# Graph layers: degrees reordered and repeated through DRAM instead of by products on TensorE

## The reference, cut to what matters

```python
# second block (_gcn_norm): degrees by target, with self-loops
deg = jax.ops.segment_sum(jnp.ones_like(col, jnp.float32), col, num_segments=n)
dis = jnp.where(deg > 0, jax.lax.rsqrt(jnp.maximum(deg, 1.0)), 0.0)
norm = dis[row] * dis[col]
...
h = x @ W
msg = h[row] * norm[:, None]
out = jax.ops.segment_sum(msg, col, num_segments=n)
return out + b
...
# third block: degrees by source, with self-loops
deg = jax.ops.segment_sum(jnp.ones(row.shape[0], dtype=x.dtype), row, num_segments=n)
dis = jax.lax.rsqrt(deg)
norm = dis[row] * dis[col]
```

## Time and profile before

| | |
|---|---|
| median of 3 runs (range) | 1376.11 us (1375.21 to 1376.53) |
| profiled execution | 1378.25 us |
| span of its profile | 1376.9 us, 26581 instructions |
| PE busy | 1333.7 us (97%) |
| DVE, ACT busy | 910.2 us (66%), 635.5 us (46%) |
| mean granted TensorE clock | 0.990 |

### The profile page before, as it was taken

How to read it: one execution, slowest core, us unless ns; L and a number is a source line. 1 busy time by engine, 2 the same in 40 slices (tenths; PEclk the granted TensorE clock), 3 DMA queues, 4 the chain that set the end, 5 groups by cost and what they waited for, 6 DMA issues and landing times.

```text
span 1376.9 us, 26581 instructions
## 1 busy us (share of the span) xinstructions
PE 1333.7 (97%) x11145; PEld 827.1 (60%) x11145; DVE 910.2 (66%) x1375; ACT 635.5 (46%) x1076; POOL 88.7 (6%) x86
## 2 busy tenths in 40 slices
PE   8789999989998999999999999999999999999998
PEld 8688899889996665544444444454444445344443
DVE  8898998999997886688668776442354323432423
ACT  2676566655654447763366334211262224422322
POOL 3120010001001210000000001011100000000000
PEclk9899999999999999999999999999999999999999
DMA  9634444344437741000000002022220323463201
GB/s 336 236 108 133 152 145 136 105 140 138 157 126 281 231 154 32 33 1 31 1 1 1 7 25 84 0 78 68 70 61 1 85 69 98 178 229 101 84 0 62
DMA packets 71335, 136.92 MB, mean 99 GB/s; under 512 B 11909, under 2 KB 24325, under 8 KB 69799
## 3 DMA queue, kind: packets, MB, share of 16 engines
q1 hardware_dynamic: 68542, 123.98, 27.3%
q0 software_dynamic: 1280, 5.77, 1.5%
q10 hardware_dynamic: 1384, 5.38, 1.1%
HBM read 81.79 MB, written 53.32 MB: 98 GB/s over the span
## 4 chain that ended last, share of the span: by engine, by line
PE 83%; DVE 12%; ACT 2%; issue 2%; DMA 1%; SPq 0%; POOL 0%; ACTq 0%; DVEq 0%; POOLq 0%
PE banks L2544 16%; PE banks L2484 14%; PE banks L2419 13%; PE banks L2606 12%; PE banks L1255 6%; PE banks L1659 4%; DVE x_sb L894 3%; PE banks L1192 3%; PE banks L1209 2%; PE banks L1266 2%; PE banks L1166 2%; DVE x_sb L877 1%; PE banks L2356 1%; PE banks L1629 1%; PE banks L1647 1%
## 5 line engine op out<-in xcount | busy, mean ns | idle before, releaser
L2544 PE MATMUL banks<-g,count 128*128 128x512 f16 x1024 | 227.5, 379 | 0.5 <-DVE tiles L2991 0.5
L2419 PE MATMUL banks<-w_parts,h_parts 128*128 128x512 f16 x960 | 217.4, 381 | 4.3 <-DVE h_parts L2694 2.4
L2544 PEld LDWEIGHTS banks<-g,count 128*128 128x128 f16 x1024 | 99.8, 98 | 113.6 <-DVE tiles L2991 1.0
L2606 PE MATMUL banks<-g,part 128*128 128x512 f16 x768 | 165.9, 379 | 0.0
L2419 PEld LDWEIGHTS banks<-w_parts,h_parts 128*128 128x128 f16 x960 | 91.3, 98 | 120.3 <-issue 11.9
L894 DVE TENSOR_TENSOR x_sb<-eb_parts,x_sb 128x4096 f16<-128x4096 f16 x64 | 145.9, 2280 | 0.0
L1255 PE MATMUL banks<-x_sb 128*128 128x128 f16 x2048 | 126.9, 221 | 11.9 <-DVE x_sb L894 11.8
L1255 PEld LDWEIGHTS banks<-x_sb 128*128 128x128 f16 x2048 | 121.0, 99 | 15.3 <-DVE x_sb L894 14.2
L2606 PEld LDWEIGHTS banks<-g,part 128*128 128x128 f16 x768 | 75.1, 98 | 90.6
L3069 DVE SCALAR_TENSOR_TENSOR part<-count,e_scale,part 128x1024 f16<-128x1024 f32 x29 | 37.2, 1284 | 105.9 <-ACT part L2306 105.9
L2306 ACT ACTIVATE part<-count,e_scale 128x1024 f16<-128x1024 f32 x29 | 33.3, 1149 | 110.9 <-PE banks L2606 110.9
(11 more groups left out here) (370 smaller groups left out, 2150.0 us busy)
## 6 DMA issues: line engine op xcount, KB each, us to landing
weight_dram<-w_new SPq DMA_DIRECT2D x60, 256.0 KB
count<-weight_dram SPq DMA_DIRECT2D x29, 512.0 KB, 7.0
qk_dram<-stage SPq DMA_DIRECT2D x64, 128.0 KB, 2.5
tiles<-x_dram SPq DMA_DIRECT2D x32, 256.0 KB, 3.5
x_dram<-tiles SPq DMA_DIRECT2D x32, 256.0 KB, 2.8
count<-in_x SPq DMA_DIRECT2D x4, 1024.0 KB, 13.5
h<-in_x SPq DMA_DIRECT2D x16, 256.0 KB, 5.2
h_dram<-h_t SPq DMA_DIRECT2D x8, 512.0 KB, 3.4
```

What stands on the lines that cost most here:

```text
L2419: mm = pe.matmul(out, m.h_parts[:, slot, zh, k], m.w_parts[:, zw, k], start=n == 0 and layer != 3, stop=n == len(passes) - 1)
L2544: mm = pe.matmul(m.agg_ps[:, b], m.count[:, i, c, block], m.g[:, i, z], start=i == 0 and z == 0, stop=i == NT - 1 and z == 1)
L2606: mm = pe.matmul(m.banks[:, b], m.part[:, n % 3, z, b * P:(b + 1) * P], m.g[:, q, gz], start=q == 0 and (z, gz) == (0, 0), stop=q == NT - ...
```

## The change

The matrices, masks and products go. The in-degrees are loaded from `deg_dram` a second time, by four loads in the order of the sums; the same three small operations as on `dis1` are done on `odis1`. `dis_by_graph` is stored to a new `dis_dram` when it is finished, and loaded back repeated over the partitions as `dis_row`. The out-degrees go to `dis_dram` from `dis2` in four-byte pieces and come back in the order of the sums by four loads; DVE takes them in (`own_degrees`, now one scaling) at the beginning of group 1 of layer 2 instead of in group 0.

```diff
@@ prep_pool
-    own = keep.own_mask[:].rearrange("p (b v) -> p b v", b=PER)
-    pool.memset(keep.own_mask[:], 1.0).then_inc(s["pool"], 1)
...
-    pool.affine_select(out=own, in_=own, compare_op=ALU.is_ge, fill=0.0, base=GPC - 1,
-                       pattern=[[0, PER], [GPC, P // GPC]], channel_multiplier=-1)
@@ attention_sp
+def by_own(values):
+
+    return values.rearrange("(c g b v) -> c v g b", c=GROUPS, g=GPC, b=PER)
...
                 sp.dma_start(keep.dis1[:], io["deg_dram"].rearrange("(t p) -> p t", p=P)).then_inc(s["in_deg"], 16)
+                for c in range(GROUPS):
+                    sp.dma_start(keep.odis1[:, c * PER:(c + 1) * PER], by_own(io["deg_dram"])[c]).then_inc(s["in_deg"], 16)
             sp.dma_start(layers.dis_by_graph[:], io["deg_dram"].rearrange("(g v) -> g v", v=GN)).then_inc(s["in_deg"], 16)
...
             load_v(slab + 2)
+    sp.wait_ge(s["dis"], 1)
+    sp.dma_start(io["dis_dram"][0].rearrange("(g v) -> g v", v=GN), layers.dis_by_graph[:]).then_inc(s["out_dis"], 16)
+    sp.wait_ge(s["out_dis"], 16)
+    sp.dma_start(layers.dis_row[:], io["dis_dram"][0:1].to_broadcast([P, N])).then_inc(s["in_dis"], 16)
@@ attention_act, attention_dve
             act.sqrt(keep.dis1[:], keep.dis1[:])
+            act.sqrt(keep.odis1[:], keep.odis1[:])
...
-            dve.wait_ge(s["in_deg"], 32)
+            dve.wait_ge(s["in_deg"], 16 * (GROUPS + 2))
...
+            dve.tensor_scalar(keep.odis1[:], keep.odis1[:], 1.0, 1.0, ALU.add, ALU.max)
...
+            dve.reciprocal(keep.odis1[:], keep.odis1[:])
@@ layers_sp, at the beginning of the sums of layer 2
+        if layer == 2:
+            sp.wait_ge(s["dis2"], 1)
+            with nc.allow_non_contiguous_dma(reason="the out-degrees to the order of the sums"):
+                sp.dma_start(io["dis_dram"][1].rearrange("(t p) -> p t", p=P), m.dis2[:]).then_inc(s["out_dis2"], 16)
+                sp.wait_ge(s["out_dis2"], 16)
+                for c in range(GROUPS):
+                    sp.dma_start(m.odis2[:, c * PER:(c + 1) * PER], by_own(io["dis_dram"][1])[c]).then_inc(s["in_dis2"], 16)
@@ layers_pool: the matrices pair and spread1 are no longer made
@@ layers_act, products of layer 0
-            if layer == 0 and 9 <= t < 9 + GROUPS:
-                c = t - 9
-                act.wait_ge(keep.attention_sems["dis_made"], c + 1)
-                act.copy(m.dis_row[:, c * COLS:(c + 1) * COLS].rearrange("p (g v) -> p g v", g=GPC),
-                         m.agg_ps[:, c].rearrange("p (v g) -> p g v", g=GPC)).then_inc(keep.attention_sems["dis_rowed"], 1)
@@ layers_pe: own_degrees, degrees and turn_own are removed
-                if layer == 0 and t == 5:
-                    own_degrees()
-                if layer == 0 and 8 <= t < 8 + GROUPS:
-                    degrees(t - 8)
...
-                pe.wait_ge(keep.attention_sems["dis_rowed"], GROUPS)
+                pe.wait_ge(keep.attention_sems["wo_done"], NT)
+                pe.wait_ge(keep.attention_sems["copied_av"], NT)
...
-            if layer == 2 and n == 52:
-                pe.wait_ge(s["dis2"], 1)
-                pe.transpose(m.dis2_row, m.dis2[:], keep.ident[:]).then_inc(s["dis2_row"], 1)
-            if layer == 2 and n == 60:
-                turn_own()
@@ layers_dve: in_degrees is removed
-        dve.wait_ge(keep.attention_sems["dis_rowed"], GROUPS)
+        dve.wait_ge(keep.attention_sems["in_dis"], 16)
...
-        dve.wait_ge(s["dis2_row"], 1)
-        dve.wait_ge(s["paired"], 2)
-        for z in range(2):
-            dve.tensor_copy(m.spread[:, z].rearrange("r c (v e) -> r c v e", e=GPC), spread_out(m.pair[:, z], NT))
-        dve.tensor_copy(m.dis2_t[:], m.dis2_row).then_inc(s["dis2_t"], 1)
-        dve.wait_ge(s["own"], 1)
-        settle(dve.tensor_tensor(m.own[:], m.own_ps, keep.own_mask[:].unsqueeze(1).to_broadcast([P, GROUPS, GN]), ALU.mult))
-        settle(dve.tensor_reduce(m.odis2[:], m.own[:].rearrange("p c (b v) -> p (c b) v", b=PER), axis=AX.X, op=ALU.add))
+
+    def own_degrees():
+
+        dve.wait_ge(s["in_dis2"], 16 * GROUPS)
         dve.tensor_scalar(m.odis2[:], m.odis2[:], m.unscale[:, 3:4], None, ALU.mult).then_inc(s["odis2"], 1)
...
+            if c == 1 and layer == 2:
+                own_degrees()
```

More of the change, by code:

```diff
@@ L217, in prep_pool @@
     pool.wait_ge(s["mask"], 1)
-    own = keep.own_mask[:].rearrange("p (b v) -> p b v", b=PER)
-    pool.memset(keep.own_mask[:], 1.0).then_inc(s["pool"], 1)
[L220 to L223, removed]
-    pool.affine_select(out=own, in_=own, compare_op=ALU.is_ge, fill=0.0, base=GPC - 1,
-                       pattern=[[0, PER], [GPC, P // GPC]], channel_multiplier=-1)
     pool.memset(keep.half_of[:], 0.0)
     pool.memset(keep.deg[:], 0.0).then_inc(s["pool"], 1)
-    pool.wait_ge(s["pool"], 7)
+    pool.wait_ge(s["pool"], 5)
     for half in range(2):
@@ L231, in prep_pool @@
         pool.memset(keep.half_of[rows, GTILES - 1 + half * GTILES:GTILES + half * GTILES], 1.0).then_inc(s["pool"], 1)
+        pool.wait_ge(s["pool"], 6 + 3 * half)
+        pool.iota(keep.d0[rows], pattern=[[1, CPT], [2 * GN, HGRAPH]], base=half * GN, channel_multiplier=0, **exact).then_inc(s["pool"], 1)
+        pool.wait_ge(s["pool"], 7 + 3 * half)
+        pool.iota(keep.iota_cnt[rows], pattern=[[1, CCOLS]], base=-half * NT, channel_multiplier=0, **exact).then_inc(s["pool"], 1)
         pool.wait_ge(s["pool"], 8 + 3 * half)
[L233 to L236, removed]
     pool.iota(keep.iota_src[:], pattern=[[1, P]], base=0, channel_multiplier=0, **exact)
     pool.iota(keep.iota_tile[:], pattern=[[1, NT], [0, 2]], base=0, channel_multiplier=0, **exact).then_inc(s["pool"], 1)
-    pool.wait_ge(s["pool"], 14)
+    pool.wait_ge(s["pool"], 12)
     pool.wait_ge(s["indexed"], 1)
@@ L1464 @@
 ATTENTION_SEMS = ("in_wo in_bo plus wo score score_read lowered exped prob turned copied_prob weighed copied_av wo_done var std normed dve "
-                  "in_qk0 in_qk1 in_v0 in_v1 out_deg in_deg deg deg_root dis own_dis dis_made dis_rowed " + " ".join(f"in_x{i}" for i in range(SLABS)) + " " + " ".join(f"out_x{i}" for i in range(4)))
+                  "in_qk0 in_qk1 in_v0 in_v1 out_deg in_deg deg deg_root dis out_dis in_dis " + " ".join(f"in_x{i}" for i in range(SLABS)) + " " + " ".join(f"out_x{i}" for i in range(4)))
 SHORT = NT - 3
@@ L1863, in layers_memory @@
     m.part = place("part", [P, 3, 2, HALF], F16, AT_Q)
-    m.spread = place("spread2", [NT, 2, GROUPS, P], F32, AT_Q)
-    m.spread1 = place("spread1", [NGRAPH, GROUPS, P], F32, AT_Q)
     m.dis_by_graph = place("dis_by_graph", [NGRAPH, GN], F32, AT_REST + 27136)
-    m.own = place("own2", [P, GROUPS, GN], F32, AT_Q + 4096)
-    m.dis2_t = place("dis2_t", [NT, P], F32, AT_Q + 5120)
-    m.pair = place("pair", [NT, 2, NGRAPH], F32, AT_Q + 5632)
     m.h_parts = place("h_parts", [P, 2, 2, KT, P], F16, AT_EB + 4096)
@@ L1968 @@
 LAYER_SEMS = ("looped in_w in_b in_all whi wlo wturned relued turned copied hi lo prod ghi glo agg fin "
-              "relu_h plus relued_sum var std normed out_sum out_root dis2 paired dis2_row dis2_t own dve phi part part_done y "
+              "relu_h plus relued_sum var std normed out_sum out_root dis2 out_dis2 in_dis2 dve phi part part_done y "
               "relued_y yfin kept joined mixed mix_used high combined out_total peak peak_row peak_one peak_all w_scaled h_scaled g_scaled b_scaled e_scaled odis1u odis2 unscaled y_scaled var_last std_last normed_last "
@@ L2424, in product @@
         mm.then_inc(s["prod"], 1)
-    def own_degrees():
-        attended = keep.attention_sems
-        pe.wait_ge(attended["dis"], 1)
-        pe.wait_ge(attended["wo_done"], NT)
-        pe.wait_ge(attended["copied_av"], NT)
-        pe.wait_ge(s["paired"], 4)
-        for c in range(GROUPS):
-            mm = pe.matmul(m.own1_ps[:, c], m.spread1[:, c], m.dis_by_graph[:], start=True, stop=True)
-        mm.then_inc(attended["own_dis"], 1)
-    def degrees(c):
-        attended = keep.attention_sems
-        pe.wait_ge(attended["dis"], 2)
-        for b in range(PER):
-            t = c * PER + b
-            mm = pe.matmul(m.agg_ps[:, c, b * P:(b + 1) * P], keep.odis1[:, t:t + 1].to_broadcast([P, P]), keep.ident[:], start=True, stop=True)
-        mm.then_inc(attended["dis_made"], 1)
     def products(layer):
@@ L2573, in between @@
             turn(2, c * PER + own.index(n))
-    def turn_own():
-        pe.wait_ge(s["dis2_t"], 1)
-        for c in range(GROUPS):
-            for z in range(2):
-                mm = pe.matmul(m.own_ps[:, c], m.spread[:, z, c], m.dis2_t[:, z * GN:(z + 1) * GN], start=z == 0, stop=z == 1)
-        mm.then_inc(s["own"], 1)
     turn(0, 2)
@@ L2878, in products @@
                 tools.last_norm()
-            if layer == 0 and t == 7:
-                in_degrees()
             if layer == 0 and t < HT:
@@ L3157, in program @@
         keep.odis1 = sb("odis1", [P, NT], F32)
-        keep.own_mask = sb("own_mask", [P, GN], F32)
```

25 lines of the change are left out of this document (3 added, 22 removed).

## The result

The changed kernel takes 1370.34 us (median of 11 runs, 1366.27 to 1373.23), the one before 1376.53 in the same comparison (11 runs, 1374.29 to 1380.53). The ratio is 0.9948, with a 95% interval of 0.9935 to 0.9962: faster by 5.2 to 8.9 us. Forecast were 1370.0 and a range of 1367.6 to 1373.4.

What follows compares the result with a forecast made beforehand. PE, busy for 97% of the span, was taken to bound the kernel. The terms -4.59 + 0.8 + 0.2 - 2.54 = -6.1 us brought the median from 1376.11 to 1370.0 us, range 1367.6 to 1373.4.

Steps and rivals of the forecast that it cites:

- PE's removed pieces in layer 0 (4.59): Products of layer 0: spreading products (1.03 us) and four sets of identity products (0.89 each) leave PE's chain, 4.59 us.
- a wait for ACT (0.8): Layer 0, transpositions 12 and 13 behind product 8: PE waits for ACT's relus, giving back 0.8 us.
- Product 15's 0.72: End of layer 0's products: PE's existing 0.72 us wait for DVE's long string stays, since that string moves up with PE.
- 0.2 for the square root: Before layer 0's first product: ACT's one added square root of a 128x16 tile was charged as 0.2 us lost.
- 2.54 in layer 2: Sums of layer 2: transposition and spreading products removed from PE (2.05 us), plus PE's 0.49 us stall at group 1.
- POOL's instructions "worth nothing": Preparation: removing POOL instructions gains 0 us, since POOL afterwards waits 27.34 us for the records.
- Outside one place both are ready early: Products of layer 0: both operand halves, from ACT and DVE, are ready before PE needs them, except at one place.
- The DMAs: Attention and layer 2: added loads and stores stay hidden; 5.2 us SP hold, 3.9 us to spare; layer 2, 9 us.
- (a): Rival, layer 0: each identity product comes back as a wait for ACT; only -3.4 us, 1372.7; chance 14%.
- (d): Rival: nothing gained in layer 0, DVE's string being fixed by something other than PE; 3.8 us at best, 1372.3; 5%.
- (b): Rival, layer 2: the path over DRAM is late; at 11.5 us of delay the 2.54 are gone, 1372.5; 7%.
- (c): Rival, attention: four-byte loads hold SP 20.7 us, PE waits 11.6 for the v slab; +5.5 us, 1381.6; 6%.

Runs made afterwards that it cites:

- products_kept: The changed kernel with PE again doing the 16 identity products behind products 7 to 10 of layer 0, unread; 1371.82 us, 0.9960 against the kernel before.
- high_later: The changed kernel with ACT's cast of a layer 0 operand moved from behind product 7 to behind product 8; 1369.60 us in one run.
- own_late: The kernel before, with DVE reading the spread out-degrees at the beginning of group 1 in layer 2, PE's products kept; 1377.50 us, ratio 0.9990.
- layer0_only: The changed kernel with the out-degrees of layer 2 handled as before; 1373.87 us, 0.9964 against the kernel before.
- two_stores: The changed kernel with the layer 2 store of the out-degrees done and waited for twice; 1371.54 us, 0.9946 against the kernel before.
- many_loads: The changed kernel with twelve more loads of 512 four-byte pieces behind the four in attention, into a spare tile; 1369.50 us, 0.9936 against the kernel before.
- wide_store: The changed kernel with the out-degrees stored in 128 pieces of 64 bytes instead of 2,048 of four; 1371.20 us, 0.9945 against the kernel before.
- pool_kept: The changed kernel with the four POOL instructions making the pair and spreading matrices put back at their old place, unread; 1366.39 us in one run.

## Why the prediction was right

The time, the sign and the mechanism came out as forecast: 1370.34 for 1370.0, and by the traces 3.93 + 2.81 = 6.74 us gained for 6.1. That the two times lie within 0.4 us is luck in part: the median of the kernel before came out at 1376.53, 1377.13 and 1378.19 in three comparisons, and the terms below are off by 0.1 to 0.3 us in both directions. The terms:

- **PE's removed pieces in layer 0 (4.59), less a wait for ACT (0.8).** The wait stands at the place and with the releaser that were named, 0.88 by its rows and 0.90 by the stretch (1.05 less the 0.15 of before), and no other place got one. products_kept and high_later show both signs of it. The prediction called the chain an unbroken run of PE pieces; it was not. It left PE for ACT before transpositions 8 and 9 in the kernel before, and does so still. Read to the letter, its last sign of being wrong, that the chain leaves PE for ACT at more places than one, came for this reason; what is new is one place.
- **Product 15's 0.72 stays.** It is 0.91, 0.19 more. The string on DVE did move up with PE, as said.
- **0.2 for the square root.** Nothing of it reaches PE. The root sets ACT's next copy back by 0.11 us, and PE's way is the same in both traces: 44.65 us from the first read of the v slab (483.49 before, 484.87 after) to the last Wo product, which lies behind the root, and 5.40 from there to the first product of layer 0.
- **2.54 in layer 2.** 2.81, of which the stall is the mis-sized part. I took the idle time that the row names, 0.49; own_late, which removes the stall alone, gives 0.68. The difference stands in the chain: behind the wait its piece of 42 matmuls takes 9.24 us (904.67), and at 0.216 each they take 9.07.
- **POOL's instructions "worth nothing".** I weighed those in the preparation and left out those at the end of attention, whose row was there to be read: a selection of 32x512 on POOL beside a subtraction of 1.01 us on DVE, where one of the same form took 0.69. That is the 0.31 at the third product. "Outside one place both are ready early" was wrong there: the product waited 0.56 us for DVE.
- **The DMAs.** All hidden, with other prices than I took. The store to DRAM 12.3 us for 6.9, the loads behind it 0.64 each to issue for 1.3, so DVE's wait was over at 909.4; taking off the 3.9 us by which layer 2 begins earlier, the first tile of group 1 came 1.5 us before my estimate, by errors that cancel: the store was 5.4 longer, the four issues 2.6 shorter, the way from the stores of group 0 to the tile 9.6 us for 13.1, and the out-degrees 0.8 earlier. The hold in attention was 6.61 for 5.2. At the end of attention the store landed after 1.8 us for 6.5, and the repeated row of 1 MB after 4.5, where two v slabs had suggested 11.6.

The rivals: (a) and (d) are excluded by products_kept and by layer0_only, (b) by the 10.4 us to spare and by two_stores. (c) did not come, and the reason that the prediction gave against it, that part of the hold was not the small pieces' own, is what many_loads shows: in its run twelve loads cost 8.40 us and four cost 8.29.

The Trainium skill's rule on transfers under 512 bytes (page "DMA: Bandwidth & Descriptors", section "Specifications") pointed the right way for the store, 12.3 us for 8 KB. But the 64-byte pieces of wide_store are under that bound as well, and took 1.4, and so are the 32 pieces of 256 bytes at the end of attention, which took 1.8: the bound alone does not tell the price.

That the profiled spans differ by 7.2 us is partly chance: a clock dip of 1.35 in the one, and 1.38 more ahead of the last Wo product in the other, at a lower clock, which cancel.

## What to carry to other kernels

When small work is taken from the bounding engine, look at what the engines beside it do at that same place: the removed time comes back where their row of work was hidden behind it, once here and for 0.88 of 4.59 us, and moving one of their operations by a step took it away again. Read the worth of such a change from one stretch between marks that both traces have; pool_kept and the changed kernel, equal but for 0.31 us, had spans of 1364.9 and 1369.7, and 4.65 us arose ahead of the last Wo product. There the granted clock was 0.91 and 0.86 in the first 60 us, and 1.00 against 0.91 and 0.83 in the stretches 240 to 260 and 290 to 300 us. Before a helper's instructions are priced at nothing, look at what the other engines' rows beside them take.

## What the runs showed of the hardware

A store of 8 KB to DRAM took 10.4 to 12.3 us in 2,048 pieces of four bytes, 1.4 us in 128 pieces of 64, and 1.8 us in 32 pieces of 256. A load of 512 four-byte pieces took 0.64 us to issue in layer 2 and 0.70 behind four of its like in attention, and 2.5 us to land. The four in attention held the queue for 6.61 and 8.29 us, where a single load had held it for 5.18. A DVE subtraction on two inputs took 1.01 us instead of 0.69 beside a selection on POOL, which itself took 1.54 instead of 1.08 where DVE had begun first. And two executions whose own stretches differ by 0.31 us had spans of 1364.9 and 1369.7 us, with a granted clock of 0.91 and 0.86 in their first 60 us.
